# A two-layer perceiver block on one core: the last expert stage in one block with rows fetched and added by transfer, and the dense layer with its norms in one block

## The reference, cut to what matters

```
# first layer, after its self attention (h is (2,256,256))
h   = layernorm(attn @ so_w + so_b + h) * so_g + so_be
ff  = gelu(h @ fi_w + fi_b) @ fo_w + fo_b          # 256 -> 1024 -> 256
x   = x + layernorm(ff + h) * fo_g + fo_be
# next sublayer starts with two norms of x
n   = rmsnorm(layernorm(x), norm_w)

# last sublayer (8 experts, hidden 1024), on layernorm(x)
scores = softmax(n @ router_w.T)                   # (2,256,8)
gate, sel = top_k(scores.T, 65)                    # 65 tokens per expert and batch
y   = gelu(n[sel] @ w1[e] + b1[e]) @ w2[e] + b2[e]
out = x + scatter_add(y * gate, sel)
```

## Time and profile before

| | |
|---|---|
| median of 3 runs | 1773.76 us (1770.83 to 1776.09) |
| the profiled execution | 1771.14 us, its span 1769.3 us |
| mean granted TensorE clock | 0.965 |
| PE busy | 1653.6 us (93%) |
| PE weight loads busy | 1002.6 us (57%) |
| DVE busy | 1136.0 us (64%) |
| ACT busy | 863.2 us (49%) |
| POOL busy | 244.8 us (14%) |
| DMA | 193.60 MB, mean 109 GB/s |

### The profile page before, as it was taken

One profiled execution on the slowest core, in us unless ns is written; L12 is line 12 of the kernel. 1 busy time (PEld: TensorE's weight loads), 2 busy tenths in 40 slices (PEclk: granted clock), 3 DMA queues, 4 the chain that ended last, 5 costly groups with the idle time before them and its releaser, 6 DMA issues. The chain is left out here.

```text
span 1769.3 us, 36593 instructions
## 1 busy us (share of the span) xinstructions
PE 1653.6 (93%) x12571; PEld 1002.6 (57%) x12579; DVE 1136.0 (64%) x1997; ACT 863.2 (49%) x1777; POOL 244.8 (14%) x323
## 2 busy tenths in 40 slices
PE   7999999999999998868999999799999999989698
PEld 3444445445454545544868999444445444546597
DVE  5777788888888856536452111388888888836311
ACT  2222227777777775512531111257777777746232
POOL 1422220000000000000202444220000000000000
PEclk9999999999999999989898999989999999999699
DMA  5578656434343408000046999654443434130052
GB/s 193 184 194 216 203 161 118 72 54 71 54 71 59 66 4 182 1 0 1 0 156 221 328 312 296 206 91 67 60 68 56 70 54 71 19 97 2 26 180 93
DMA packets 145830, 193.60 MB, mean 109 GB/s; under 512 B 27593, under 2 KB 119260, under 8 KB 139712
## 3 DMA queue, kind: packets, MB, share of 16 engines
q1 hardware_dynamic: 139064, 188.30, 43.6%
q0 software_dynamic: 4608, 2.18, 0.8%
q10 hardware_dynamic: 2064, 1.87, 0.3%
HBM read 155.42 MB, written 39.97 MB: 110 GB/s over the span
## 5 line engine op out<-in xcount | busy, mean ns | idle before, releaser
L1280 ACT ACTIVATE probs<-ps 128x512 f32<-128x512 f32 x1024 | 558.5, 599 | 181.4 <-PE ps L1186 169.0
L1306 DVE TENSOR_REDUCE top<-ps 128x1 f32<-128x1024 f32 x504 | 594.1, 1220 | 61.6 <-PE ps L1165 48.8
L1186 PE MATMUL ps<-qst,kst 105*128 105x256 bf16 x2048 | 353.9, 276 | 6.9 <-DVE qst L1311 1.5
L1165 PE MATMUL ps<-kst,qst 105*128 105x512 bf16 x1008 | 307.7, 388 | 5.3 <-DVE top L1306 3.5
L1186 PEld LDWEIGHTS ps<-qst,kst 105*128 105x128 bf16 x2048 | 170.2, 100 | 227.5 <-ACT probs L1280 86.4
L1200 PE MATMUL ps_o<-probs,vst 128*32 128x256 f32 x4096 | 274.1, 385 | 2.3 <-ACT probs L1280 2.3
L1200 PEld LDWEIGHTS ps_o<-probs,vst 128*32 128x32 f32 x4096 | 106.8, 109 | 113.3 <-issue 51.2
L2219 PE MATMUL ps_h<-xe,vall 128*128 128x80 f32 x1024 | 155.2, 273 | 0.0
L2219 PEld LDWEIGHTS ps_h<-xe,vall 128*128 128x128 f32 x1024 | 142.0, 199 | 0.0
L395 POOL COPY vst<-vall 128x512 f32 (+1 forms) x64 | 39.4, 616 | 698.0 <-PE ps_o L1200 695.2
L1165 PEld LDWEIGHTS ps<-kst,qst 105*128 105x128 bf16 x1008 | 88.6, 99 | 64.4 <-issue 29.0
(11 more groups left out here) (397 smaller groups left out, 2026.7 us busy)
## 6 DMA issues: line engine op xcount, KB each, us to landing
kst<-kd SPq DMA_DIRECT2D x372, 128.0 KB
kd<-probs SPq DMA_DIRECT2D x64, 384.0 KB, 2.8
vall<-in_L_ffn_wg_dram SPq DMA_DIRECT2D x32, 512.0 KB
vall<-in_L_ffn_wu_dram SPq DMA_DIRECT2D x32, 512.0 KB
vall<-in_L_ffn_wd_dram SPq DMA_DIRECT2D x32, 512.0 KB
w<-in_L_ffn_w_dram SPq DMA_DIRECT2D x16, 1024.0 KB, 5.6
vd<-square_weights SPq DMA_DIRECT2D x16, 512.0 KB, 4.1
vall<-vd SPq DMA_DIRECT2D x16, 512.0 KB, 6.0
```

The costliest lines, as they stand in the source:

```text
L1165: mm = pe.matmul(ps1[:, slot1(m, u), x * 512:(x + 1) * 512], qst[:, m, qt * P:(qt + 1) * P], kst[:, m, c * W1 + x * 512:c * W1 + (x + 1) * ...
L1186: mm = pe.matmul(ps2[:, SCORES2[u], x, :], kst[:, m, kt * P:(kt + 1) * P], qst[:, m, :], start=True, stop=True)
L1280: nc.scalar.activation(probs[:, u % SLOTS, :, :], ps2[:, SCORES2[u], :, :], ACT.Exp).then_inc(probs_ready, 1)
L1306: v.tensor_reduce(top[:, b, qt, c:c + 1], ps1[:, slot1(m, u), :], AX, ALU.max).then_inc(mx, 1)
```

## The change

**Dense stretch.** The projection, the empty block, `dense_ffn` and both `norm_phase` calls become one block. The projection and the first norm are as in `project_and_normalize`, but ACT adds epsilon as the bias of its square root, from a column that GpSimd sets first. The hidden tiles are made for one half of the tokens at a time (256 columns, three PSUM buffers); the first half starts when its two tiles are normalized. Two hidden tiles of the second half come before the first two output tiles. GpSimd adds biases, shift and residual ahead. DVE takes each output tile through both remaining norms by itself; the RMS norm's root is taken from the layer norm's variance, so no second statistics of the normalized values are needed. ACT's order is: copies, roots of the first norm, all GELUs, roots of the other two.

**Last expert stage.** Router, experts and store become one block. The router's weights are loaded transposed by two transfers. As in `experts0`, `xn` is stored to memory (`xrows`), token numbers and shares come from a table, in two groups (experts 0 and 1, then 2 to 7), GpSimd fetches the rows of each expert and batch (65 rows of 1 KB, four experts ahead), and PE transposes them. The bias product plus the residual is stored to the output (`orows`) as a base; each expert's output is scaled by its share and added there by an accumulating indirect transfer, batch by batch, each after the previous addition of the same batch has landed. The up projection has four PSUM buffers instead of two. There are 16 filler matmuls before the first expert. No store follows.

```
 # dense_ffn, one block
+            @block.gpsimd
+                g.memset(eps[:, 0:1], LN_EPS).then_inc(eps_set, 1)
+                g.memset(eps[:, 1:2], RMS_EPS * LN_EPS).then_inc(eps_set, 1)
+                for t in range(NT):
+                    g.tensor_tensor(added[:, 0, t, :], xn[:, t, :], bias[:, :], ALU.add).then_inc(bias_added, 1)
+                for t in range(NT):
+                    g.tensor_tensor(shifted[:, t, :], x[:, t, :], out_shift[:, :], ALU.add).then_inc(next_added, 1)
+                for t in range(NT):
+                    pool.wait_ge(done, t + 1)
+                    g.tensor_tensor(added[:, 1, t, :], xn[:, t, :], fo_b[:, :], ALU.add).then_inc(next_added, 1)
 # PE, after the projection
+                for t in range(2):
+                    stay_busy(ps_x[:, 1, :, :].rearrange("p c n -> p (c n)"), 3)
+                    turn_normed(t, done, x_turned)
+                stay_busy(ps_x[:, 1, :, :].rearrange("p c n -> p (c n)"), 3)
+                pe.wait_ge(loading[0], loading[1])
+                pe.wait_ge(x_copied, 1)
+                for f in range(NF):
+                    hidden(0, f)
+                    if f in (1, 3):
+                        turn_normed(2 + f // 2, done, x_turned)
+                pe.wait_ge(x_copied, 2)
+                for f in range(AHEAD):
+                    hidden(1, f)
+                out(0)
+                out(1)
+                for f in range(AHEAD, NF):
+                    hidden(1, f)
+                out(2)
+                out(3)
+                for t in range(NT):
+                    stay_busy(ps_t[:, 0, :], 3)
+                    turn_normed(t, n_done, n_turned)
 # ACT
+                act.wait_ge(eps_set, 2)
 ...
+                for f in range(NF):
+                    gelu(1, f)
+                for t in range(NT):
+                    for i in range(1, 3):
+                        root(i, t)
+                    if t % 2:
+                        copy_x(t // 2, n_turned)
 # DVE, after the first norm
+                for t in range(2):
+                    out_moments(t)
+                    centre(1, t, total, centred, out_gain)
+                for t in range(2):
+                    add_to_x(t)
+                    centre(2, t, other, scaled, rms)
+                for t in range(2):
+                    normalize_both(t)
+                for t in range(2, NT):
+                    out_moments(t)
+                    centre(1, t, total, centred, out_gain)
+                    add_to_x(t)
+                    centre(2, t, other, scaled, rms)
+                    normalize_both(t)
 # experts1, one block
+    GROUPS = ((0, 2), (2, E1))
+    YB = 4
+    NH = 4
+    TURN_Y_AT, TURN_X_AT, COPY_X_AFTER = 1, 3, 5
 # SP
+                sp.dma_start(xrows.rearrange("(t p) d -> p t d", p=P), xn[:, :, :]).then_inc(rows_out, 16)
+                sp.wait_ge(base_ready, 1)
+                sp.dma_start(orows.rearrange("(t p) d -> p t d", p=P), base[:, :, :]).then_inc(base_out, 16)
+                for e in range(E1 - 2):
+                    sp.wait_ge(h_made, FT1 * (e + 1))
+                    buffers.load_w1(sp, e + 2)
+                    sp.wait_ge(y_made, e + 1)
+                    buffers.load_w2(sp, e + 2)
 # GpSimd
+                pool.wait_ge(base_out, 16)
+                for e in range(E1):
+                    if e + XB1 < E1:
+                        pool.wait_ge(x_turned, e + 1)
+                        fetch(e + XB1)
+                    for b in range(B):
+                        pool.wait_ge(y_copied, B * e + b + 1)
+                        if e >= 1:
+                            pool.wait_ge(y_added[b], 16 * e)
+                        nc.gpsimd.indirect_dma_start(
+                            orows, bass.IndirectOffsetOnAxis(token[:, e, b:b + 1], 0), ye[:, e % YB, b, :], None,
+                            bounds_check=N - 1, oob_is_err=False, compute_op=ALU.add).then_inc(y_added[b], 16)
 # PE, after the slots
+                table(0)
+                pe.wait_ge(gated, 1)
 ...
+                mm.then_inc(bias_made, 1)
+                table(1)
+                for _ in range(BUSY_MATMULS):
+                    pe.matmul(ps_y[:, :, :].rearrange("p c w -> p (c w)"), pr.cb("identb"), pr.constsb[:, 0:C * W],
+                              start=True, stop=True)
+                turn_x(0)
+                pe.wait_ge(base_ready, 1)
+                for e in range(E1):
+                    for f in range(FT1):
+                        up(e, f)
+                        if f == TURN_Y_AT and e:
+                            turn_y(e - 1)
+                        if f == TURN_X_AT and e + 1 < E1:
+                            turn_x(e + 1)
+                    down(e)
+                turn_y(E1 - 1)
 # DVE
+                for j in range(len(GROUPS)):
+                    one_hot(j)
+                    slots_of(j)
+                dve.wait_ge(bias_made, 1)
+                v.tensor_tensor(base[:, :, :], acc, residual[:, :, :], ALU.add).then_inc(base_ready, 1)
```

More of the change, by code:

```diff
@@ L201, in loading_of @@
     return (loaded, 16 * len(names)), issue
[L204 to L210, removed]
 def load_start(pr, l0):
@@ new lines, in _ @@
+                mm.then_inc(sc_t, 1)
+                pe.wait_ge(taken_ready, 1)
+                for q in range(QT):
+                    mm = pe.transpose(ps_c[:, q, :], taken[:, q * P:(q + 1) * P], pr.cf("ident")[0:EB, 0:EB])
+                mm.then_inc(taken_t, 1)
+                pe.wait_ge(chosen_ready, 1)
+                for t in range(NT):
+                    first = t - t % QT
+                    for u in range(first, t + 1):
+                        mm = pe.matmul(ps_n[:, t, :], pr.cb("earlier") if u == t else pr.cb("ones"), chosen[:, u, :],
+                                       start=(u == first), stop=(u == t))
@@ L2727, in expert, with copy_x @@
-                def expert(e, b, place):
+                def copy_x(e):
+                    act.wait_ge(x_turned, e + 1)
+                    nc.scalar.copy(xe[:, e % 2, :, :], ps_x[:, :, :]).then_inc(x_copied, 1)
+                act.wait_ge(ex, 1)
+                nc.scalar.activation(score[:, :, :], score[:, :, :], ACT.Exp).then_inc(ex, 1)
+                copy_x(0)
+                for e in range(E1):
                     for f in range(FT1):
-                        act.wait_ge(h_made, FT1 * e + f + 1)
-                        if f == 0 and place not in ("first", "second"):
+                        n = FT1 * e + f
+                        act.wait_ge(h_made, n + 1)
+                        if f == 0 and e >= 2:
@@ L2753, in _ @@
                 v = nc.vector
[L2755 to L2766 removed]
+                link = Chain(dve, steps)
@@ new lines, in _ @@
+                dve.wait_ge(ex, 2)
+                link(v.tensor_reduce(sm[:, :], score[:, :, :], AX, ALU.add))
+                link(v.reciprocal(mx[:, :], sm[:, :]))
+                link(v.tensor_tensor(score[:, :, :], score[:, :, :], bc(mx[:, :], 2, E1), ALU.mult))
+                dve.wait_ge(both_ready, 1)
+                for b in range(B):
+                    last = v.tensor_copy(both[:, :, 32 * b:32 * b + E1], score[:, b * QT:(b + 1) * QT, :])
+                last.then_inc(both_ready, 1)
```

689 lines of the change are left out of this document (325 added, 364 removed).

## The result

| | median us | runs | lowest to highest |
|---|---|---|---|
| before | 1773.76 | 4 | 1770.83 to 1776.09 |
| changed | 1732.01 | 4 | 1730.64 to 1735.45 |

The ratio is 0.9768, 95% interval 0.9748 to 0.9789. By the medians that is 41.8 us less, where 47.2 were summed up. Set against a kernel before that was run again beside it, the same changed kernel later came to 1726.73 against 1769.86 us, ratio 0.9752 (0.9737 to 0.9767). The first changed execution that was profiled took 1730.64 us around a span of 1728.8.

What follows compares the result with a forecast made beforehand. Serial DVE work was taken to bound the dense stretch, TensorE the experts behind a serial start. Gains of 19.5 and 27.7 us sum to 47.2, giving 1723.9 or 1726.6, stated as 1725 us; 8-in-10 range 1714 to 1741.

Steps and rivals of the forecast that it cites:

- rival 4: Expert stage: waits for additions into the output make the kernel slower, 1780 us if a round takes 15 us; chance 0.03.
- signs of being wrong: An expert over 9 us, PE waiting on transfers, or projection block to clamped attention over 52 us.
- First hidden matmul at 742.5: Dense block: the first half's hidden matmuls start at 742.5 us instead of 747.04.
- the two cancel: Dense block's start: 0.35 us wait for GpSimd's memsets offsets about 0.15 us saved per tile of DVE's chain.
- VectorE's wait and its tail: Dense block: DVE waits until 766.1 us for the first root, then finishes the output tiles at 779.4 us.
- Gain of 19.5 us: Dense stretch: next stage's first matmul at 780.8 us instead of 800.29; bounds 14 and 23 us.
- Expert 0 starts 26.3 us in: Last expert stage: expert 0 starts at 1665.6 us instead of 1663.97, a loss of 1.6; bounds 1664.4 and 1668.5.
- landing of 1.6 us: Before expert 0: fetched rows land 1.6 us after GpSimd's transfer; the other bound was 5.3 us.
- 8.07 us per expert: Experts: each takes 8.07 us instead of 11.56, without gather and combination; 63.7 us over the stage, PE the bound.
- the microsecond of clock that was not lost: Expert 0: of 5.0 us lost at the lower clock, 1.0 was kept in the sum; bounds 0 and 5.
- The end, 11.3 us, no gain: After the last down projection: 11.3 us where it took 11.4, the store gone but more semaphores cleared.
- The terms written down, 7.1 and 4.0: Kernel's end: 7.1 us for copy, transposes, scaling, additions and landing; 4.0 us for 61 semaphore clears.

Runs made afterwards that it cites:

- e5: The changed kernel run again with nothing altered, beside the kernel before in another group of runs: 1726.73 us.
- e11: The changed kernel without loading the weights of experts 2 to 7, which compute with those of 0 and 1: 1730.68 us (two runs).
- e1: The kernel before with only the new dense block; second expert stage and store stay old: 1756.13 us, ratio 0.9916.
- e3: The changed kernel with the token fetches of experts 2 and 3 issued only after all eight hidden tiles of expert 0 are made: 1726.55 us.
- e7: The changed kernel with 6 instead of 16 filler matmuls before expert 0's tokens are turned: 1727.01 us, ratio 0.9764.
- e10: The changed kernel with the experts' rows written over the output's rows instead of added to them: 1733.36 us (two runs).
- e9: The changed kernel with GpSimd's four sums of x and the second shift moved behind the four sums after the first norm: 1728.94 us.
- e6: The changed kernel with ScalarE's copy of the first two turned token tiles behind the first root of tile 2, not ahead: 1724.02 us.
- e12: The changed kernel with semaphores cleared together, that copy behind the root, and GpSimd's sums of x and second shift later: 1726.86 us, ratio 0.9755.
- e2: The kernel before with only the second expert stage and store new; old dense layer and norms stay: 1744.96 us, ratio 0.9860.
- e4: The changed kernel with the semaphores released at the very end cleared together, 8 instructions instead of 61: 1724.11 us, ratio 0.9733.
- e8: The changed kernel with semaphores cleared together after every stage that runs once, and ScalarE's copy behind the first root of tile 2: 1722.13 us.

## Why the prediction was nearly right

The direction, the range (1714 to 1741) and the mechanism held: both stretches lost what was said, TensorE stayed the bound of the experts, and no rival decided (rival 4 needed landings of over 12 us, and in e5 the additions landed within 7.2). The forecast of 1725 was 7 us too low for the first measurement and 2 us for the second. One of its own signs of being wrong did appear: expert 0 took 13.3 us in the first trace, over its limit of 9, though not because of the later weights' loads (e11).

That the total came so near is in part luck. Set against e5, which has no gaps, four steps of the sum miss by 1.2 to 2.1 us and cancel: the dense block is 49.5 us for 48.3, the start of expert 0 24.5 for 26.3, the experts 63.0 for 64.7 and the end 13.4 for 11.3, together 150.4 for 150.6.

The first step below needs one more row, the dense block's first matmuls in e5 (timeline), beside their 1.09 us in the first trace:

```profile
732.43 0.63 PE L1589 MATMUL ps_t<-consts,attn 128*128 128x128 f32 x4 [0.89 <-PEq L1315]
```

- **First hidden matmul at 742.5, 10.0 us in.** It was 10.9 us in (10.4 in e1, e3 to e7, e10 and e11). The half microsecond between them is the clock: the block's first four transposes took 1.09 us in the first trace, where the granted clock was 0.54, and 0.63 in e5, where it was 1.00. The other 0.4 is the step that failed, "the two cancel": the tile chain was priced by instructions that ran alone, and GpSimd's sums, counted as hidden because they end in time, slowed VectorE's by 0.15 to 0.33 us each. e9 gives 0.5 us back (9.83).
- **VectorE's wait and its tail.** The wait for the first root ended 34.5 us in (33.6 forecast, the start's 0.9). The tail from there took 15.5 us, forecast 14.7; the missing 0.9 is ScalarE's copy ahead of a root, which e6 shows. Tile lengths were right: 4.8 for the first two together (5.0 forecast), 4.1 for the last (4.14).
- **Gain of 19.5 us.** 17.8 in the first trace, 15.5 as the runs time it. The larger part of this miss is the length of the old block, 67.8 us in one trace and 65.0 in the other: 2.7 us were one execution's stretch at 1.2 GHz. I read one trace and took its clock for the kernel's.
- **Expert 0 starts 26.3 us in.** 24.1 to 25.7. Most of this miss stands ahead of the fetch: the slots were ready 15.3 us in (1637.72 + 0.19 - 1622.57), where 17.7 less 0.6 were forecast. The scoring product alone is 1.6 us shorter than in the trace I read, 1.92 for 3.51, and again by the clock. The landing of 1.6 us was right (1.54 in e7), where the Trainium skill's rule, "DMA: Bandwidth & Descriptors", "Anatomy of one DMA", gave an estimated 2.15. The fillers were, as said, what sets the start; they took 3.2 us for 3.5.
- **8.07 us per expert.** 7.90: turning the fetched rows takes 0.25, not 0.45 us. Times eight, and with the microsecond of clock that was not lost, the experts took 62.7 to 63.0 instead of 64.7 us.
- **The end, 11.3 us, no gain.** 12.9 to 13.4 with the 61 clears and the additions. (The terms written down, 7.1 and 4.0, add up to 11.1.) The clears were right (4.2 for 4.0), and so was everything until GpSimd's last instruction ends (5.7 us for 5.5). From there to the first clear 3.3 us pass, where I had 1.6: 1.75 for the landing and 1.5 for the end of the block, that is SyncE's wait and the engines' meeting, which I left out.
- **What no step foresaw**: the gaps in expert 0, 5.5 us with the slower matmuls behind them. How much of the 5.3 us between 1732.0 and 1726.7 they make is not shown, as the kernel before moved by 3.9 us between the same groups. In the traces that have them TensorE's signals reach ScalarE and SyncE 3 to 6 us after the matmuls' recorded starts, for the second half of the hidden tiles. Excluded by runs, as the gaps stay without them: the loads of the later weights (e11), the addition in the transfer (e10), the single clears (e12). Excluded as the only cause: the program itself, which ran with them and without (e5). Open: whether GpSimd's eight fetches in a row are needed for it, since e3 ran where the gaps did not occur, and what differs between the groups of runs.

In sum, without the gaps: the old parts in their second traces (65.0 in e2, 128.1 in e1) less the new ones (49.5 and 100.9 in e5) give 15.5 + 27.2 = 42.7 us, where the medians of e5's group are 43.1 apart. The first trace of before gives 18.3 + 29.1 = 47.4, close to my 47.2: the sum reproduced the execution that it was read from. Of the 4.7 us between the two, 2.7 are the hidden layer's matmuls and 1.6 the scoring product, both at a lower clock than in the second trace.

## What to carry to other kernels

Before you credit a change with the clock that a stretch lost, look whether a second execution of the same kernel loses it there too; the window at 0.84 was one execution's, and no property of the kernel. When a forecast comes out, compare its steps too: here four of them missed and cancelled. A helper engine whose work "ends in time" can still slow the engine beside it, so price both with the rows of instructions that run together. At the end of a kernel count everything behind the last transfer: landing, the block's end, and each semaphore that is cleared by itself.

## What the runs showed of the hardware

- A stage's length can depend on the group of runs: 62.7 to 63.0 us in two groups (e7 apart), 68.1 to 69.9 in two others, the changed kernel among both. The kernel before had medians of 1773.8 and 1771.4 us in the groups with the gaps and of 1771.1 and 1769.9 in those without.
- An indirect transfer that adds takes GpSimd 1.45 us to issue, a plain one 0.93, and they differ little in landing (at the least 1.75 and 1.4 us). Beside the weights' loads the additions land later, 6.0 us after the start of their issue in the median, for 3.3 without the loads (e11).
- VectorE's instructions with two operands in SBUF took 0.63 to 0.78 us beside GpSimd's sums and 0.45 to 0.49 without them (e5, the changed kernel, e9).
- The same matmuls run at either level from one execution to the next: 16.69 and 13.97 us (before, e2), 3.51 and 1.95 (before, e1), 1.09 and 0.63 (changed, e5).
- A pause of 0.94 us and ten fewer filler matmuls left the following 16 instructions at 1.2 GHz (3.81 us for 2.03, e7).
- 61 single clears take 4.2 us, 8 or 9 joined ones with their drains 1.5 to 1.7 (e4, e8).
